# A transformer block on one core: one written-out TensorE order over two head groups, operand loads merged from eight to four, and layer-norm work moved to GpSimd

## The reference, cut to what matters

```
x = x + attn(layernorm(x))        # x is (8, 512, 128)
    q, k, v = (y @ W.T + b) split into 16 heads of 8
    softmax(q k^T / sqrt(8)) * head_mask, times v, @ Wo.T + bo
x = x + moe(layernorm(x))
    shared = gelu(y @ Wfc_s + bfc_s) @ Wproj_s + bproj_s
    top 2 of 8 experts by softmax(y @ Wr), weights made to sum to 1
    routed = sum over the two of weight * (gelu(y @ Wfc[e] + bfc[e]) @ Wproj[e] + bproj[e])
```

## Time and profile before

| | us |
|---|---|
| median of 3 runs | 681.98 (677.87 to 686.18) |
| the profiled execution | 682.79 |
| its span (first to last instruction) | 681.0 |
| outside the span | 1.8 |

### The profile page before, as it was taken

One profiled execution on the slowest core, in us unless ns is written; L12 is line 12 of the kernel. 1 busy time (PEld: TensorE's weight loads), 2 busy tenths in 40 slices (PEclk: granted clock), 3 DMA queues, 4 the chain that ended last, 5 costly groups with the idle time before them and its releaser, 6 DMA issues. The chain is left out here.

```text
span 681.0 us, 15669 instructions
## 1 busy us (share of the span) xinstructions
PE 636.6 (93%) x5218; PEld 394.5 (58%) x5218; DVE 498.9 (73%) x1075; ACT 411.1 (60%) x950; POOL 260.7 (38%) x461
## 2 busy tenths in 40 slices
PE   7888999999999999999999989999999999999998
PEld 4444444444444444444444444444689999998966
DVE  6986567897788788788888877952646666666647
ACT  4654556675676676676676676677435555555651
POOL 5303330131063163163163162264665455545510
PEclk7995559999899899899899898999999999999999
DMA  6776122232234212112112211100122222222164
GB/s 191 246 278 217 38 65 55 73 96 78 79 97 111 77 50 64 49 49 60 53 51 57 55 49 49 34 18 21 59 64 67 67 65 63 68 60 66 52 230 157
DMA packets 41127, 57.53 MB, mean 84 GB/s; under 512 B 11002, under 2 KB 24186, under 8 KB 41066
## 3 DMA queue, kind: packets, MB, share of 16 engines
q1 hardware_dynamic: 36746, 47.86, 23.9%
q0 software_dynamic: 4320, 8.89, 3.9%
HBM read 33.66 MB, written 22.52 MB: 83 GB/s over the span
## 5 line engine op out<-in xcount | busy, mean ns | idle before, releaser
L964 DVE TENSOR_REDUCE mx<-ps 128x2 f32<-128x1024 f32 x256 | 309.1, 1216 | 82.7 <-PE ps L1384 81.0
L830 ACT ACTIVATE probs<-ps 128x512 f32<-128x512 f32 x512 | 263.2, 607 | 115.2 <-PE ps L1410 107.9
L1410 PE MATMUL ps<-q_op,k_op 35*128 35x512 f32 x512 | 190.7, 502 | 28.9 <-ACT probs L830 23.4
L1410 PEld LDWEIGHTS ps<-q_op,k_op 35*128 35x128 f32 x512 | 77.7, 194 | 141.1 <-ACT probs L830 99.4
L1424 PE MATMUL ps<-probs,v_op 128*32 128x256 f32 x2048 | 159.2, 429 | 0.0
L1384 PE MATMUL ps<-k_op,q_op 33*128 33x512 f32 x512 | 153.4, 453 | 3.2 <-DVE mx L964 2.4
L888 ACT ACTIVATE probs<-ps,b_cur 128x128 f32<-128x128 f32 x284 | 80.9, 368 | 68.0 <-PE ps L1629 53.8
L1424 PEld LDWEIGHTS ps<-probs,v_op 128*32 128x32 f32 x2048 | 66.8, 119 | 62.9 <-ACT probs L830 26.2
L714 POOL DMA_INDIRECT results<-rest,row_id x71 | 73.2, 1030 | 73.5 <-DVE rest L1265 55.8
L605 POOL DMA_INDIRECT slots<-route_sb,slot_u x64 | 64.4, 1006 | 89.1 <-ACT probs L830 78.3
L1629 PE MATMUL ps<-xn,w_cur 128*128 128x128 f32 x568 | 77.9, 280 | 1.5 <-ACT probs L888 1.2
(11 more groups left out here) (172 smaller groups left out, 536.2 us busy)
## 6 DMA issues: line engine op xcount, KB each, us to landing
q_op<-q_scr SPq DMA_DIRECT2D x128, 64.0 KB, 2.7
k_op<-k_scr SPq DMA_DIRECT2D x128, 64.0 KB, 2.7
w_sb<-in_W SPq DMA_DIRECT2D x18, 256.0 KB
probs<-slots SPq DMA_DIRECT2D x71, 64.5 KB
q_scr<-probs SPq DMA_DIRECT2D x8, 512.0 KB, 4.0
k_scr<-probs SPq DMA_DIRECT2D x8, 512.0 KB, 4.3
k_scr<-probs SPq DMA_DIRECT2D x8, 256.0 KB, 4.6
k_op<-results SPq DMA_DIRECT2D x4, 512.0 KB, 5.1
```

The source lines that it names most:

```text
L830: nc.scalar.activation(probs[:, i, j, :], ps[:, BANK["key", b, hg, s], :], ACT.Exp, scale=float(D) ** -0.5).then_inc(s_exp, 1)
L964: nc.vector.reduce_max(mx[:, slot % 2, :, p], ps[:, bank:bank + 2, :], AX.X).then_inc(s_max, 1)
L1410: nc.tensor.matmul(ps[:, bank, :], k_op[hg][at:at + rows, j, P * i:P * (i + 1)], q_op[hg][at:at + rows, j, :], start=True, stop=True).then ...
```

## The change

The TensorE order of two head groups is now one string of 64 letters (K a key score, R a pair of row scores, H one half of a P.V product); the halves run four behind the groups (`PV_LAG`). A half can stand alone between scores. In a pair of row scores the half of the array that goes first is the one that the key score before it didn't use. The eight operand loads of a group become four of 128 KB: source and destination cover both 16-row blocks, in the source as an outermost dimension of 2 (with step 0 for q, which is read twice). GpSimd normalises the fourth to eighth sequence instead of the fourth alone, and does its other first-stage work between and behind. DVE's `out_norm` steps move one pair earlier.

```diff
-        N_LD, N_SH = 8, 2
+        N_LD, N_SH = 4, 2
-        PV_AT = ((3, 3, 4, 5), (2, 3, 4, 5))
+        ORDER_PE = "RKKRKHKRKHKKRKHHKRKKRHKKRKHHRKKK" "RHHKRKKHKRKRKHHKRKKHRKKHKRKRKHHK"
+        PV_LAG = 4
...
-                    for r in range(PARTS):
-                        for scr, op, first in ((q_scr, q_op, 0), (k_scr, k_op, D * r)):
-                            src = scr[b, :, :].rearrange("(x h) t -> x h t", h=H)[first:first + PR, head:head + JH, :]
-                            sp.dma_start(op[hg][at + PR * r:at + PR * (r + 1), :, :].bitcast(f32), src).then_inc(s_ld[hg], 16)
+                    for scr, op, shift in ((q_scr, q_op, 0), (k_scr, k_op, D)):
+                        seq = scr[b, :, :]
+                        src = bass.AP(tensor=seq.tensor, offset=seq.offset + head * S,
+                                      ap=[[shift * H * S, PARTS], [H * S, PR], [1, JH * S]])
+                        to = op[hg][at:at + KR, :, :].bitcast(f32).rearrange("x j t -> x (j t)")
+                        sp.dma_start(to, src).then_inc(s_ld[hg], 16)
...
+            normalise(POOL_SEQ)
+            ln1_rstd(3)
+            zero_scores(3)
+            normalise(POOL_SEQ + 1)
...
+            for b in range(POOL_SEQ + 2, B):
+                normalise(b)
+            max_split(0)
...
-                if b + 2 < B and b + 2 != POOL_SEQ:
+                if b + 2 < POOL_SEQ:
                     normalise(b + 2)
...
-                        if p >= 4 and hg == 2:
-                            out_norm(b, 0, p - 4)
+                        if 3 <= p < 7 and hg == 2:
+                            out_norm(b, 0, p - 3)
...
-                for half in range(2):
+                for half in (first, 1 - first):
...
+            def product_half(n):
+
+                if 0 <= n < NG * 2 * NT:
+                    g, i = n // (2 * NT), n // 2 % NT
+                    pv(g // HG, g % HG, i, n % 2)
...
+            def attend(b, two):
+
+                g = b * HG + 2 * two
+                key, row, half, due = 0, 0, 2 * NT * g - PV_LAG, None
+                for op in ORDER_PE:
+                    if due is not None and op == "K":
+                        more(*due)
+                        due = None
+                    if op == "K":
+                        at = b, 2 * two + key // (J * NT), key % (J * NT)
+                        key_scores(*at)
+                        key, due = key + 1, at
+                    elif op == "R":
+                        for s in (2 * (row % PAIRS), 2 * (row % PAIRS) + 1):
+                            if (b, 2 * two + row // PAIRS, s) in ROWS:
+                                pair = ROWS[b, 2 * two + row // PAIRS, s]
+                                row_scores(pair // (HG * PAIRS), pair // PAIRS % HG, pair % PAIRS, key % 2)
+                        row += 1
+                    else:
+                        product_half(half)
+                        half += 1
```

More of the change, by code:

```diff
@@ L1133, in attend @@
                             last_max_out()
-                        if p >= 4 and hg == 2:
-                            out_norm(b, 0, p - 4)
-                        elif p >= 4 and hg == 0 and not first:
-                            out_norm(b - 1, 1, p - 4)
+                        if 3 <= p < 7 and hg == 2:
+                            out_norm(b, 0, p - 3)
+                        elif 3 <= p < 7 and hg == 0 and not first:
+                            out_norm(b - 1, 1, p - 3)
                         if not first:
@@ L1374, in project_v, with row_scores @@
                 last.then_inc(s_vp, 1)
-            def row_scores(b, hg, p):
+            def row_scores(b, hg, p, first=0):
                 j, i, rows = p // NT, p % NT, KR + 1
@@ L1428, in pv @@
                     last.then_inc(s_pv, 1)
-            def products(b, hg, quad):
-                for i in range(NT):
-                    if PV_AT[(hg - 1) % 2][i] == NT + quad and b * HG + hg > 0:
-                        for half in range(2):
-                            pv((b * HG + hg - 1) // HG, (hg - 1) % HG, i, half)
-                for i in range(NT):
-                    if PV_AT[hg % 2][i] == quad:
-                        for half in range(2):
-                            pv(b, hg, i, half)
+            def product_half(n):
+                if 0 <= n < NG * 2 * NT:
+                    g, i = n // (2 * NT), n // 2 % NT
+                    pv(g // HG, g % HG, i, n % 2)
             def max_rows(b, hg):
@@ L1563, in _, with more @@
-            sequences(attend)
-            for i in range(NT):
-                if PV_AT[(HG - 1) % 2][i] >= NT:
-                    for half in range(2):
-                        pv(B - 1, HG - 1, i, half)
+            def more(b, hg, s):
+                for kind, *which in extras(b, hg, s):
+                    if kind == "mx":
+                        max_rows(*which)
+                    elif kind == "project":
+                        project_out(*which)
+                    elif kind == "yT":
+                        transpose_y(*which)
+                    elif kind == "logitsT":
+                        logits_by_expert(*which)
+                    elif kind == "logits":
+                        logits_out(*which)
+                    else:
+                        ranks(*which)
@@ new lines, in attend @@
+            def attend(b, two):
[15 more added lines that the diff above has]
+                        row += 1
+                    else:
+                        product_half(half)
+                        half += 1
+                        if due is not None:
+                            more(*due)
+                            due = None
+                if due is not None:
+                    more(*due)
@@ L1569, in _ @@
+            for b in range(B):
+                for two in range(HG // 2):
+                    attend(b, two)
+            for n in range(NG * 2 * NT - PV_LAG, NG * 2 * NT):
+                product_half(n)
             pe.wait_ge(s_wffn, 16 * N_WFFN)
```

52 lines of the change are left out of this document (8 added, 44 removed).

## The result

The changed kernel takes 805.46 us (median of 4 runs, 790.74 to 824.24), the kernel before 679.92 (675.26 to 686.18, 4 runs beside them): 1.171 times the time, 95% interval 1.153 to 1.189. This ratio, like those of the experiments, leaves out the executions more than 1.5% above the fastest of their kernel, which ran at a lower clock; by the medians it is 1.185. The profiled execution took 797.3 us; its span is 795.5.

What follows compares the result with a forecast made beforehand. No engine was full: each stops while another works, and DVE would come to set the pace. 682.8 + 19.3 (first stage) - 11.7 (groups) - 2.0 (last three groups) + 0 (half clock) = 688.4 us, said as 688; 8-in-10 range 650 to 745.

Steps and rivals of the forecast that it cites:

- Two engines: Operand loads: a source beginning with a dimension of 2 runs on two engines only, 10.3 us a group, bound 15.5.
- First stage: Before attention: loads queued between stores delay the first key score by 19.3 us, to near 71 us.
- The order: Attention groups: shorter P.V blocks end standstills, 11.6 us a group for 12.88; alone 33 us gained in the middle part.
- these two signs: Attention: DVE's wait for row scores down from 58 us, and no 3.6 us standstill of ACT.
- The mode changes of the array: TensorE block edges: draining at tiling changes costs 0.1 us an edge; with 4 more blocks TensorE needs 10.3 us a group.
- A: Whole kernel: the prediction's main case, as its sum says, 676 to 702 us with the clock's bounds; chance 0.45.
- The groups with two-engine loads: Attention groups: shift rows wait behind loads, 12.8 us against 11.6; mean 12.43 us a group, 11.7 us gained over 26.
- The half clock: Start of attention: three groups at 1.2 GHz cost the same, 0, with bounds of -8 and +11 us.
- Rival B: Loads on two engines become the bound: 740 us at 13 us a load, 813 at 15.5; chance 0.25.
- C: Operand loads use all engines after all: 648 us, 640 to 660; chance 0.15.
- D: Loads on two engines, hidden by groups of 11.6 us, so only the first stage pays: 667 us; chance 0.15.
- GpSimd's part: First stage: normalising moved from ACT to GpSimd is worth nothing under the delay, without it at most 2 us.

Runs made afterwards that it cites:

- e3: Changed kernel with the loads' two outer source dimensions exchanged, so they use all 16 engines: 701.13 us, no ratio.
- e1: Changed kernel with the eight old loads, new TensorE order and GpSimd work kept: 672.92 us, x 1.005.
- h2: e1 with two idle DMA round trips ahead of the shift rows: 807.91 us, 1.18 by the medians.
- h3: Kernel before, its order and eight loads, with three idle DMA round trips ahead of the shift rows: 806.28 us, x 1.185.
- h1: e1 with one idle DMA round trip ahead of the shift rows: 700.62 us, no ratio.
- e2: Kernel before with only the four new two-engine loads: 726.39 us, x 1.063.
- h4: f4 with the loads of one half of the heads on two engines: 652.78 us, x 0.960.
- f4: e3 with one block of four P.V halves in every second head group: 646.61 us, x 0.965.
- e4: Kernel before with only GpSimd's normalising of the fourth to eighth sequence moved: 684.67 us.
- g4: f4 with ScalarE normalising the fifth to eighth sequence again, as in the kernel before: 635.74 us, x 0.960.
- g3: f4 with the kernel before's eight loads in place of the four 16-engine loads: 633.89 us, x 0.955.
- g2: Changed kernel with 16-engine loads and P.V in four blocks of four halves per two groups, out_norm at its earlier pair: 742.14 us, x 1.123.
- f3: Changed kernel with shift rows issued from ScalarE's queue, not SP's behind the loads: 826.51 us, no ratio.
- f2: e3 with one block of four P.V halves in each head group: 674.43 us, x 0.985.

## Why the prediction was wrong, step by step

**Two engines: right.** Eight small packets a group, 11.3 us of packets on each of two engines for a predicted 10.3 (within the bounds of 10.3 to 15.5), so 0.177 us a packet for 0.161. e3 shows that the leading dimension of 2 does it. The Trainium skill's DMA: Bandwidth & Descriptors, section Rules for kernel authors, has the rule, and the profile after agrees.

**First stage: right.** 19.3 us predicted, 21.7 measured; first key score at 73.3 us for 71.

**The order: right in size, where the clock was up.** I had 11.6 us a group without the loads; e1 has 11.4 at full clock, and behind its first rise ScalarE's longest wait for key scores there is 2.4 us, where it was 3.7. In the changed kernel these two signs failed, because of what follows: VectorE waited 130.6 us for row scores in the middle part, not under 58, and ScalarE still stood 3.6 us. The mode changes of the array that the Trainium skill, TensorEngine Tiling (Array Packing), section Key Properties, warns of did not show as a cost beyond that sum. Two slips of the prediction change nothing here: three exponentials last 3 x 0.607 = 1.8 us, not 1.5, which speaks for the order still more, and A's 676 to 702 is 680 to 699 with the clock's bounds as given.

**The groups with two-engine loads: right as a mechanism; that the totals agree is chance.** The forecast was 12.43 us a group for 11.6, so 26 x 0.83 = 21.6 us of standing, and TensorE stood 22.3 us. But it stood ten times, 0.7 to 3.9 us each, not 26 times for 0.5 to 1: at 1.2 GHz a group takes 19.7 us and mostly hides the loads' 12.8, so that nine of the ten stops fell into the stretches at full clock.

**The half clock: this step failed.** "Three such groups cost the same: 0", with bounds of -8 and +11 us, priced the start of attention alone. That start did cost nothing (48.0 us at 0.50 after, 52.7 at 0.51 before). The error was to leave the clock of the other 26 groups as it had been, while the same sum put a stop in front of most of them. Rival B had the words, "standing TensorE lets the clock fall more often", but no price, and tied them to slower packets. What the runs showed in place of the 0: 327 us of attention at 1.2 GHz for 76, each fall behind the first rise next to a stop, and h2 and h3 get the same loss from stops alone, with the old loads.

The price closes the sum in hindsight; how much time at 1.2 GHz the stops bring has to be taken from each trace. e1 without its time at 1.2 GHz: 413.5 - (2 x 0.16 x 413.5 = 132) x (18.9 - 11.4)/18.9 = 361 us. On this base, with 0.40 us lost per us at 1.2 GHz and the stops added:

| | attention, us | at 1.2 GHz, us | stops, us | 361 + 0.40 x cold + stops |
|---|---|---|---|---|
| e3 | 459.2 | 248 | 0.6 | 461 |
| h1 | 425.3 | 153 | 3.1 | 425 |
| changed kernel | 511.6 | 327 | 22.3 | 514 |
| h2 | 517.9 | 342 | 18.6 | 516 |

All four have the changed order; the two terms behind the base explain the whole. Against the kernel before's 420.5 us of attention that is -59 (the order, all of it at full clock), +131 (clock) and +22 (stops), 94 for 91 measured. To compare with the prediction, the kernel before's own 76 us at 1.2 GHz have to come out as well: at the same 0.40 that is 30 us, which leaves -29 for the order, +101 for the clock and +22 for the stops (an estimate; the old order may lose less per us). I had -35, 0 and +22, so the clock's term is nearly all of what was missing.

**Why loads and order hurt more together.** A stop needs the shift rows to be late. Between their issue and the next group's first key score the old order has, in every second group, its long P.V block (four halves) directly ahead of that score; the new one has a block of one half and one of two there. SyncE's and TensorE's rows ahead of the eighteenth group, the kernel before first (timeline, 276.5 to 286 us), then e1 (257 to 262.3 us):

```profile
276.96 1.27 SPq L369 DMA_DIRECT2D q_op<-mxT  x2
...
281.50 3.44 PE L1424 MATMUL ps<-probs,v_op 128*32 128x256 f32 x32
284.87 0.63 PE L1410 MATMUL ps<-q_op,k_op 35*128 35x512 f32 x2
```

```profile
257.24 1.27 SPq L370 DMA_DIRECT2D q_op<-mxT  x2
...
261.17 0.64 PE L1409 MATMUL ps<-q_op,k_op 35*128 35x512 f32 x3
```

7.9 us pass there between issue and use, 4.2 here (the group's key score is the second of the three, at 261.41). Some 1.5 of the 7.9 is the long block at half clock, 3.44 us for the 1.93 of the earlier trace rows. Over eight groups, the thirteenth to the twentieth, it is 6.1 to 7.9 and 4.2 to 5.8. e2, with the old order's slack, stood 6.2 us; the changed kernel 22.3. The runs show both halves of it: give either order stops (h2, h3), and each loses over 120 us; take the stops away and leave the loads partly on two engines (h4), and three executions of five lose nothing.

**The rivals.** B's far end, 813 us, lies near the result by chance: it needs 15.5 us a load. By B's own rule the measured 11.3 gives groups of 12.3 us and a first stage 22 us longer, some 688 us in all. C (all engines, 640 to 660 us) holds for e3's best run, 638.7, and for f4, but not for e3's median of 701: the order alone keeps the clock low in some executions. D was excluded by the stops. GpSimd's part made no difference that can be told, as said (e4, g4).

**What stays open.** Why e3 ran at 712 us and at 639 in the same lot, why the kernel before has long falls in some executions (e4's profiled one, the old order too) and what decides how long a fall lasts in a given order (7, 20, 44 or 89 us), no run isolates. That P.V laid out in one block in two groups mostly keeps the clock up and in two a group doesn't is shown by f4, g3, g4 and g2; with none the four runs of e3 and of e1 lie between. The reason is only read off stretches such as g2's. f3 settles nothing.

## What to carry to other kernels

Price a stop of TensorE not by its length but with the time at 1.2 GHz that follows it: here 19 to 22 us of stops, half a us to 4 us each, came with some 200 us more at 1.2 GHz behind them than e1 had, at 0.40 us lost per us. But don't take that as a fixed rate: f3 lost more behind smaller stops, and e1 and e3 had long falls with none. Before a schedule is tightened, list what its slack was hiding, small round trips above all, and check each against the new gap. And look at the number of small completion packets of a merged DMA: two where sixteen are wanted is an outer dimension to exchange, in one line.

## What the runs showed of the hardware

- The same matmuls, with no stop for a DMA behind the first group's, ran at a mean clock over the whole execution of 0.947 to 0.973 (f4, six runs), 0.877 to 0.940 (f2, six), 0.825 to 0.949 (e3, four) or 0.808 to 0.824 (g2, six). On TensorE nothing but the places of the P.V halves differs between them; in g2 VectorE's `out_norm` stands one pair later too. Times went from 0.965 (f4) to 1.123 (g2) of the kernel before.
- A fall without any stop for a DMA lasted 88.7 us in e1, TensorE being busy for 88.5 of them; the only wait in the 6 us ahead of it was one of 0.36 us for VectorE.
- Falls to 1.2 GHz began during a stop of TensorE for a DMA, of 0.6 to 3.9 us, or at most 2.5 us behind one: 6 of 6 in the changed kernel, 11 of 12 in h2, 13 of 13 in h3, counted behind the start of attention. Not every such stop had a fall behind it.
- Loads whose leading dimension is 2 kept two engines busy for 11.3 us per 524 KB; the same bytes with a leading dimension of 16 let attention start 24 us earlier (49.3 us in e3, 73.3 in the changed kernel), by that one line.
